# Down products of a feed-forward in three fp32r passes, their operands split on ACT and VectorE

## The chip, the cores and the metric

One core of one Trainium2 chip runs one program: a small perceiver layer, in fp32 throughout. The metric is the device time of one execution in microseconds, the median of several. The engines are PE (TensorE, the matrix engine), DVE (VectorE), ACT (ScalarE), POOL (GpSimd) and SP (SyncE, which issues DMAs here). Each runs its own instructions in order and waits for semaphores that the others raise.

## What is computed

The input `x` is 8 x 64 tokens of 512 numbers. Three blocks follow one another, each added to its input: a cross attention to a context of 8 x 1601 rows; a block with a differential attention over the heads of each token and a feed-forward; a mixture of 32 experts. The change lies in the feed-forward of the second block, whose core is:

```python
h = _layernorm(x, ln1_g, ln1_b)
src2 = _diff_attn(h, Wq, Wk, Wv, lq1, lq2, lk1, lk2, Wo, bo)
conn = skip + src2
skip2 = conn
h2 = _layernorm(conn, ln2_g, ln2_b)
src3 = jax.nn.relu(h2 @ W1.T + b1) @ W2.T + b2
return skip2 + src3
```

`W1` leads from 512 to 2048 numbers ("up"), `W2` back from 2048 to 512 ("down").

## The kernel before

The 512 tokens are 4 tiles of 128. `queries_and_cross_attention` computes the first block, and with it the attention of the second block for tiles 0 to 2. `last_head_and_feed_forward` then has two strands at once: that attention for tile 3 (the "last head"), and the feed-forward for all four tiles. `route_and_experts` follows behind a barrier of all engines.

**The last head.** PE makes `q`, `k` and `v` of tile 3, and ACT copies them out. 24 products follow (`NQ` = 16 of `q` with `k`, `NA` = 8 of the attention weights with `v`), each 128x1024, each reduced by DVE (`reduce`). Two of three products are computed by POOL (`product`, three buffers, so that product m waits for the reduction of m - 3 of its own), one by DVE itself (`vprod`). Between the 16 and the 8 stands a softmax: DVE (`z1`, maxima), ACT (`Exp`), DVE (sums, `rinv`, `rlam`), POOL (`w01`, `att2`). Behind the 8 come a mean square, `on` on POOL, its transposes and product on PE (`turn_o(3)`, `put_out(3)`).

**The feed-forward.** For tile t, DVE adds the attention's output and computes statistics (`connect(t)`), then the normalised rows `cn` (`connection_normed(t)`). PE transposes them (`turn_c(t)`), and ACT scales them into `cT` (`turned_c(t)`). `up(n)`, for n = 16 t + f, makes the f-th 128 hidden numbers of tile t with four fp32 products of 128x128; four of them fill a bank of PSUM. ACT turns a bank into `fT` with four relus (`hidden(n)`), in a ring of 8 places. `down(n)` is one fp32 product of 128x512, with `fT[:, n % 8]` as the stationary operand and a slab of `W2` as the moving one. 16 of them add up to a tile's output, and DVE adds them to `x` (`second_skip(t)`).

**The order** is written out by hand for each engine. PE runs n from 0 to 69: `up(n)`, then `down(n - 6)` (`LAG`), with `turn_c(1)`, `turn_c(2)`, `turn_o(3)`, `put_out(3)` and `turn_c(3)` put in at n = 6, 18, 34, 37 and 43. DVE runs the 24 reductions with `connect` and `connection_normed` of tiles 0 and 1 and `connect(2)` between the first; `connection_normed(2)` stands behind the softmax's maxima, those of tile 3 at the end.

**Memory.** Thirteen weight slabs of 1 MB are loaded once: 0 is `W_O`, 1 to 3 are `Wq`, `Wk` and `Wv` of the last head, 4 is `Wo`, the odd ones from 5 are parts of `W1` and the even ones from 6 parts of `W2`. Slabs 1 to 8 lie in a region called `spare`, 9 to 12 in `h_late`. Elsewhere the kernel has long used three fp32r passes in place of an fp32 product (`mm3`): each operand is split into a high part, rounded to fp32r, and a low part, what that leaves; high x high, high x low and low x high are added up.

Of the kernel before, what the change touches and what calls it, by code (L numbers as in the profile page):

```python
# [19 lines left out]
P = 128  # L20
# [3 lines left out]
TT = T // P  # L24
# [1034 lines left out]
def last_head_and_feed_forward(nc, a, keep):  # L1059
# [12 lines left out]
    with ExitStack() as ctx:  # L1072
# [6 lines left out]

        late = sb("h_late", [P, 4, KD, D])  # L1080
        row, row_loaded = keep["rows"], keep["row_loaded"]
        cols2, b1 = sb("h_cols2", [P, 2, KD]), sb("h_b1", [P, FT])
# [7 lines left out]
        cT = sb("h_cT", [P, 2, KD, P])  # L1090
        fT = sb("h_fT", [P, NF_, P])
        ps = ctx.enter_context(nc.psum_tensor("ps_h", [P, 8, 512], F32))
        UP = 5
# [20 lines left out]
        cT_full, cT_done, up_full, f_done = sem("h_cT_full"), sem("h_cT_done"), sem("h_up_full"), sem("h_f_done")  # L1114
        down_full, skip_done, x2_done = sem("h_down_full"), sem("h_skip_done"), sem("h_x2_done")

        block = ctx.enter_context(nc.Block())
# [80 lines left out]
        def _(act):  # L1198
# [15 lines left out]
            def turned_c(t):  # L1214
# [6 lines left out]
                ins.then_inc(cT_done, 1)  # L1221

            def hidden(n):
                f = n % FT
                act.wait_ge(up_full, n - f % 4 + 4)
                if n >= NF_:
                    act.wait_ge(down_full, n - NF_ + 1)
                c = slice(P * (f % 4), P * (f % 4) + P)
                nc.scalar.activation(fT[:, n % NF_], ps[:, UP + n // 4 % 2, c], ACT.Relu, bias=b1[:, f:f + 1]).then_inc(f_done, 1)

            for t in range(HT):
                turned_o(t)
            act.wait_ge(n_step, 5)
            nc.scalar.activation(std2[:, :, HT:], var2[:, :, HT:], ACT.Sqrt).then_inc(n_std_done, 1)
# [5 lines left out]
            query_key(0)  # L1240
            query_key(1)
            act.wait_ge(qkv_full, 3)
            nc.scalar.copy(v.rearrange("p d h -> p h d"), ps[:, 4].rearrange("p (h d) -> p h d", h=H2)).then_inc(qkv_done, 1)
            act.wait_ge(c_loaded, 32)
            std_second(0)
            turned_c(0)
            std_second(1)
            for n in range(4 * FT):
# [21 lines left out]
        def _(dve):  # L1270
            def reduce(n):
                what, i = kind(n)
                out, width = (att, 4 * H2) if what == "qk" else (o, 4 * D2)
                if n in by_pool:
                    m = by_pool.index(n)
                    summed = prod[:, m % NP]
                    dve.wait_ge(prod_done, m + 1)
                else:
                    m = by_vector.index(n)
                    summed = vprod[:, m % NPV]  # L1280
                    if m >= NPV:
                        dve.wait_ge(red_done, by_vector[m - NPV] + 1)
                    operands_ready(dve, n)
                    multiply(nc.vector, n, summed).then_inc(vprod_done, 1)
                    dve.wait_ge(vprod_done, m + 1)
                nc.vector.tensor_reduce(out[:, width * i:width * i + width], summed.rearrange("p (a d) -> p a d", d=D2), AX.X,
                                        ALU.add).then_inc(red_done, 1)

            def normed_once(t):
# [50 lines left out]
            connect(0)  # L1340
            normed_once(HT)
            for n in range(NQ):
                reduce(n)
                if n == 0:
                    connection_normed(0)
# [4 lines left out]
                if n == 7:  # L1350
                    connect(2)

            dve.wait_ge(red_done, NQ)
# [16 lines left out]
            dve.wait_ge(rsum_step, 2)  # L1370
            nc.vector.tensor_scalar(rlam[:], rinv[:, H2:], lam[:], None, ALU.mult).then_inc(rsum_step, 1)
            for n in range(NQ, NQ + NA):
                reduce(n)
            dve.wait_ge(sq_done, 1)
            nc.vector.tensor_reduce(ms[:], sq.rearrange("p (a d) -> p a d", a=H2), AX.X, ALU.add).then_inc(ms_step, 1)
# [4 lines left out]
            dve.wait_ge(rms_done, 1)  # L1380
            nc.vector.reciprocal(rrms[:], rms[:]).then_inc(ms_step, 1)
            connect(3)
            connection_normed(3)
            second_skip(1)
            second_skip(2)
            second_skip(3)

        @block.tensor
        def _(pe):
# [59 lines left out]
            def down(n):  # L1449
# [8 lines left out]
                if f % 4 == 0:  # L1458
                    pe.wait_ge(w_loaded[6 + 2 * (f // 4)], 16)
                pe.wait_ge(f_done, n + 1)  # L1460
                nc.tensor.matmul(bank, fT[:, n % NF_], weight(6 + 2 * (f // 4))[:, f % 4], start=False, stop=(f == FT - 1)
                                 ).then_inc(down_full, 1)

# [618 lines left out]
def build(nc, a):  # L2082
# [7 lines left out]
    with ExitStack() as ctx:  # L2090
# [5 lines left out]
        with ExitStack() as own:  # L2096
# [28 lines left out]
            keep["w_loaded"] = [nc.alloc_semaphore(f"h_w_loaded{i}") for i in range(NSLAB)]  # L2125
            keep["x_loaded"], keep["tiles_loaded"] = nc.alloc_semaphore("h_x_loaded"), nc.alloc_semaphore("h_tiles_loaded")
            queries_and_cross_attention(nc, a, keep)
            last_head_and_feed_forward(nc, a, keep)
# [63 lines left out]
```

## Time and profile before

| | us |
|---|---|
| median of 3 runs | 1512.81 |
| lowest and highest | 1511.21, 1514.98 |
| the profiled execution in all | 1515.2 |
| its span in the trace | 1513.1 |
| PE busy in the span | 1439.7 |
| DVE busy | 929.3 |
| POOL busy | 655.9 |
| ACT busy | 630.6 |

The profile is of one execution; all times below are microseconds from the start of its span. `last_head_and_feed_forward` takes from about 1001 to 1170. L numbers are lines of the kernel before. A row of the timeline gives the start, the time to the end of its last instruction, the engine and line, the operation and its operands (out<-in), the count, and in brackets how long the engine had been idle before it and who released it. An fp32 product is recorded as two matmuls, so "x2" is one down product and "x8" one `up`. Matmuls overlap in the records: the pace is read from one start to the next.

### The profile page before, as it was taken

Reading aid. Unit: us, or ns where it says so; the run is one execution under the profiler, and the core shown is the slowest. Engines: PE = TensorE matmul, PEld = TensorE weight load, DVE = VectorE, ACT = ScalarE, POOL = GpSimd, SP = SyncE. Lnnn points to the kernel's source line nnn. Section 1 sums busy time; section 2 is a strip of 40 time slices with the busy share of each in tenths; the row PEclk is TensorE's granted clock in tenths of the full one; section 3 lists DMA queues with packets and bytes.
Section 4 is the critical chain, followed back from the end, with each engine's and each line's share of the span. In section 5 each row is a group of like instructions: output and inputs, shape, how many; then the busy total and the mean of one; then the engine's idle time right before and its main releaser. Section 6 shows DMA issues by size and latency. Waiting matters only on the chain. (4 is left out here: it accounts for less than half of the span.)

```text
span 1513.1 us, 24256 instructions
## 1 busy us (share of the span) xinstructions
PE 1439.7 (95%) x8998; PEld 1223.4 (81%) x8998; DVE 929.3 (61%) x2102; ACT 630.6 (42%) x1067; POOL 655.9 (43%) x320
## 2 busy tenths in 40 slices
PE   5999999999999999999999999879999999999993
PEld 4999999989899989899998999845666556777772
DVE  6455555544487655478674459757800557888884
ACT  3344345354343444433534434422211125666662
POOL 5006006005284712464930636427600037888873
PEclk9999999999999999999999999989999799999997
DMA  5102003013002012100201300270000579999999
GB/s 200 64 5 91 1 5 127 2 38 119 29 5 89 11 67 95 60 4 23 77 32 70 107 14 1 98 305 2 1 1 2 199 300 281 370 365 367 370 365 316
DMA packets 63975, 176.96 MB, mean 117 GB/s; under 512 B 15110, under 2 KB 32006, under 8 KB 54028
## 3 DMA queue, kind: packets, MB, share of 16 engines
q1 hardware_dynamic: 53708, 151.57, 27.0%
q0 software_dynamic: 10176, 24.12, 6.5%
q8 instruction: 64, 1.05, 0.3%
q14 instruction: 27, 0.22, 0.0%
HBM read 156.00 MB, written 19.66 MB: 116 GB/s over the span
## 5 line engine op out<-in xcount | busy, mean ns | idle before, releaser
L65 PE MATMUL ps_x<-wkv_hi,c_hi 128*128 128x256 f32 (+1 forms) x832 | 241.2, 290 | 0.0
L294 POOL TENSOR_TENSOR c_hi<-c_raw,ones 128x1608 fp32r<-128x1608 f32 x31 | 90.0, 2904 | 344.7 <-DMA c_raw<-ctxT 344.7
L67 PE MATMUL ps_x<-wkv_hi,c_lo 128*128 128x256 f32 (+1 forms) x832 | 234.2, 282 | 0.0
L66 PE MATMUL ps_x<-wkv_lo,c_hi 128*128 128x256 f32 (+1 forms) x832 | 234.2, 281 | 0.0
L769 DVE TENSOR_TENSOR pT<-ps_x,pT 128x512 fp32r<-128x512 f32 (+1 forms) x224 | 145.2, 648 | 123.2 <-ACT pT L617 120.5
L65 PE MATMUL ps_x<-c_hi,wkv_hi 128*128 128x402 f32 x512 | 195.7, 382 | 3.0 <-POOL c_lo L297 2.4
L617 ACT CAST pT<-ps_x 128x512 fp32r<-128x512 f32 (+1 forms) x224 | 124.5, 556 | 167.4 <-PE ps_x L472 164.3
L598 ACT CAST vv<-ps_x 128x512 fp32r<-128x512 f32 (+1 forms) x112 | 62.1, 555 | 278.5 <-PE ps_x L67 278.5
L67 PE MATMUL ps_x<-c_hi,wkv_lo 128*128 128x402 f32 x512 | 177.9, 347 | 0.0
L66 PE MATMUL ps_x<-c_lo,wkv_hi 128*128 128x402 f32 x512 | 177.7, 347 | 0.0
L65 PEld LDWEIGHTS ps_x<-wkv_hi,c_hi 128*128 128x128 f32 (+1 forms) x832 | 153.5, 184 | 17.0 <-issue 17.0
L739 DVE TENSOR_TENSOR vv<-ps_x,vv 128x512 fp32r<-128x512 f32 (+1 forms) x112 | 72.9, 651 | 139.3 <-ACT vv L598 139.3
L313 POOL TENSOR_TENSOR x_tok<-t_q,t_k 128x1024 f32<-128x1024 f32 x48 | 114.2, 2399 | 100.8 <-PE ps_x L524 58.0
L67 PEld LDWEIGHTS ps_x<-wkv_hi,c_lo 128*128 128x128 f32 (+1 forms) x832 | 153.6, 185 | 0.0
L66 PEld LDWEIGHTS ps_x<-wkv_lo,c_hi 128*128 128x128 f32 (+1 forms) x832 | 153.2, 184 | 0.0
L487 PE MATMUL ps_x<-pT,vv 128*128 128x256 f32 (+1 forms) x832 | 138.1, 287 | 4.8 <-DVE pT L769 4.5
L733 DVE SCALAR_TENSOR_TENSOR kT_lo<-ps_x,bk,kT_hi 128x402 fp32r<-128x402 f32 x128 | 81.1, 635 | 95.7 <-ACT kT_hi L592 95.3
L487 PEld LDWEIGHTS ps_x<-pT,vv 128*128 128x128 f32 (+1 forms) x832 | 125.9, 189 | 10.5 <-DVE pT L769 7.6
L752 DVE TENSOR_SCALAR_CACHE_REDUCE prob<-ps_x 128x402 f32<-128x402 f32 (+1 forms) x256 | 131.1, 569 | 0.0
L472 PE MATMUL ps_x<-ident,prob 128*128 128x128 f32 (+1 forms) x832 | 127.8, 273 | 0.0
L297 POOL TENSOR_TENSOR c_lo<-c_raw,c_hi 128x1608 fp32r<-128x1608 f32 x31 | 115.3, 3720 | 2.4
L1697 POOL DMA_INDIRECT acc<-e_mix,e_row_out x42 | 96.0, 2286 | 34.6 <-issue 31.4
(322 smaller groups left out, 3063.3 us busy)
## 6 DMA issues: line engine op xcount, KB each, us to landing
e_gu_raw<-w_gu SPq DMA_DIRECT2D x49, 1024.0 KB
c_raw<-ctxT SPq DMA_DIRECT2D x32, 804.0 KB
e_w_dn<-w_dn SPq DMA_DIRECT2D x48, 512.0 KB
x_tok<-slabs SPq DMA_DIRECT2D x13, 1024.0 KB, 4.8
spare<-slabs SPq DMA_DIRECT2D x8, 1024.0 KB, 11.2
h_late<-slabs SPq DMA_DIRECT2D x4, 1024.0 KB, 16.6
e_mix<-shared SPq DMA_DIRECT2D x2, 1536.0 KB, 8.7
wkv_raw<-w_qkv SPq DMA_DIRECT2D x2, 1024.0 KB, 12.4
```

The source lines that it names most:

```text
L65: nc.tensor.matmul(out, a_hi, b_hi, start=start, stop=False)
L66: nc.tensor.matmul(out, a_hi, b_lo, start=False, stop=False)
L67: return nc.tensor.matmul(out, a_lo, b_hi, start=False, stop=stop)
L294: nc.gpsimd.tensor_tensor(c_hi[:, :, chunk(c)], c_raw[:, :, chunk(c)], ones[:, 0:1].unsqueeze(2).to_broadcast([P, KD, CW]), ALU.mult).then ...
L297: nc.gpsimd.tensor_tensor(c_lo[:, :, chunk(c)], c_raw[:, :, chunk(c)], f32(c_hi[:, :, chunk(c)]), ALU.subtract).then_inc(split_done, 1)
L313: nc.gpsimd.tensor_tensor(slab[:, 2 * D * (i % 2):2 * D * (i % 2) + 2 * D].rearrange("p (a b d) -> p a b d", a=2, b=2 * H2), q[:, 2 * i:2 ...
L472: ins = nc.tensor.transpose(ps[0:r, 6 + n % 2, c:c + P], prob[:, 2 * g + j, P * st:P * st + r], ident[:])
L487: ins = nc.tensor.matmul(ps[:, 4 + g, 256 * j:256 * j + 256], vv[0:r, st, 2 * g + j].rearrange("p l c -> p (l c)"), pT[0:r, n % 2, st % 2, ...
L617: nc.scalar.copy(pT[0:r, n % 2, 0:w, :, 0].rearrange("p a j c -> p (a j) c"), ps[0:r, 6 + n % 2, 0:256 * w].rearrange("p (a c) -> p a c", ...
L752: ins = nc.vector.tensor_scalar(prob[:, p, CW * n:CW * n + w], ps[:, 2 * (i % 2) + j, 0:w], 0.0, None, ALU.add, ALU.max, accum_out=pmax[:, ...
L769: nc.vector.tensor_tensor(pT[0:r, n % 2, 0:w, :, 1].rearrange("p a j c -> p (a j) c"), ps[0:r, 6 + n % 2, 0:256 * w].rearrange("p (a c) -> ...
L1697: nc.gpsimd.indirect_dma_start(out=a[f"acc{r % 2}"], out_offset=bass.IndirectOffsetOnAxis(ap=row_out[:, r % U:r % U + 1], axis=0), in_=y[: ...
```

## The change

The 64 down products become `mm3`, 192 fp32r passes. For that:

- Each of the four slabs of `W2` is split once. ACT copies it to `down_hi` (`split_down`, 128x2048), DVE subtracts (`down_lo`). `down_lo` takes the slab's own place. Three of the `down_hi` take the places of slabs 1 to 3, `Wq`, `Wk` and `Wv`, as soon as their products are done (`qkv_full`); the fourth has a place of its own.
- `fT` is split in groups of four: ACT copies four tiles to `fT_hi` behind the four relus, DVE subtracts them to `fT_lo` (`hidden_low(G)`, 128x512), G = 0 to 15.
- `down(n)` waits, at the first of each four, for `down_lo` and for `fT_lo` of its group, no longer for the single relu.

Its core, with the new waits and all places of the new calls:

```diff
+        down_hi = [down_hi_0] + [keep["down_hi"][i] for i in range(3)]
+        down_lo = [keep["down_lo_6"], keep["down_lo_8"]] + [
+            nc.alloc_sbuf_tensor_at(f"h_down_lo_{s}", [P, KD, D], F32R, offset=late_at + 4 * KD * D * (s - 9)) for s in (10, 12)]
...
+            def split_down(i):
+                if i:
+                    act.wait_ge(qkv_full, i)
+                act.wait_ge(w_loaded[6 + 2 * i], 16)
+                nc.scalar.copy(down_hi[i][:], weight(6 + 2 * i)).then_inc(down_hi_done, 1)
...
                 nc.scalar.activation(fT[:, n % NF_], ps[:, UP + n // 4 % 2, c], ACT.Relu, bias=b1[:, f:f + 1]).then_inc(f_done, 1)
+                if f % 4 == 3:
+                    s = slice(n % NF_ - 3, n % NF_ + 1)
+                    act.wait_ge(f_done, n + 1)
+                    nc.scalar.copy(fT_hi[:, s], fT[:, s]).then_inc(f_hi_done, 1)
 
             for t in range(HT):
                 turned_o(t)
+            split_down(0)
...
             query_key(0)
             query_key(1)
+            split_down(1)
...
             std_second(0)
             turned_c(0)
+            split_down(2)
+            split_down(3)
             std_second(1)
...
+            def split_down(i):
+                dve.wait_ge(down_hi_done, i + 1)
+                nc.vector.tensor_tensor(down_lo[i][:], weight(6 + 2 * i), f32(down_hi[i][:]), ALU.subtract).then_inc(down_lo_done, 1)
+
+            def hidden_low(G):
+                s = slice(4 * (G % 2), 4 * (G % 2) + 4)
+                dve.wait_ge(f_hi_done, G + 1)
+                nc.vector.tensor_tensor(fT_lo[:, s], fT[:, s], f32(fT_hi[:, s]), ALU.subtract).then_inc(f_lo_done, 1)
...
             normed_once(HT)
+            split_down(0)
             for n in range(NQ):
                 reduce(n)
+                if n in (0, 2, 4):
+                    split_down(n // 2 + 1)
                 if n == 0:
                     connection_normed(0)
...
+                if n in (5, 9, 12):
+                    hidden_low((5, 9, 12).index(n))
...
+            hidden_low(3)
             for n in range(NQ, NQ + NA):
                 reduce(n)
+                if n in (NQ, NQ + 3):
+                    hidden_low(4 + (n - NQ) // 3)
+            hidden_low(6)
...
             nc.vector.reciprocal(rrms[:], rms[:]).then_inc(ms_step, 1)
+            hidden_low(7)
+            hidden_low(8)
             connect(3)
+            hidden_low(9)
             connection_normed(3)
             second_skip(1)
-            second_skip(2)
+            for G in range(10, 4 * TT):
+                hidden_low(G)
+                if G == 12:
+                    second_skip(2)
             second_skip(3)
...
                 if f % 4 == 0:
-                    pe.wait_ge(w_loaded[6 + 2 * (f // 4)], 16)
-                pe.wait_ge(f_done, n + 1)
-                nc.tensor.matmul(bank, fT[:, n % NF_], weight(6 + 2 * (f // 4))[:, f % 4], start=False, stop=(f == FT - 1)
-                                 ).then_inc(down_full, 1)
+                    pe.wait_ge(down_lo_done, f // 4 + 1)
+                    pe.wait_ge(f_lo_done, n // 4 + 1)
+                mm3(nc, bank, fT_hi[:, n % NF_], fT_lo[:, n % NF_], down_hi[f // 4][:, f % 4], down_lo[f // 4][:, f % 4],
+                    False, f == FT - 1).then_inc(down_full, 1)
```

The engines' rows show where the new instructions stand. First DVE, from the first reduction of the last head to `cn` of tile 1 (`h_prod` are POOL's products, `h_vprod` DVE's, `h_y` the connection's sum), before:

```order
L1286 TENSOR_REDUCE t_att<-h_prod 128x64
L1307 RECIPROCAL h_crstd<-h_cstd 128x1
L1311 TENSOR_SCALAR h_cn<-h_y,h_cmv,h_crstd 128x512
L1286 TENSOR_REDUCE t_att<-h_prod 128x64
L1137 TENSOR_TENSOR h_vprod<-t_q,t_k 128x1024
L1286 TENSOR_REDUCE t_att<-h_vprod 128x64
L1286 TENSOR_REDUCE t_att<-h_prod 128x64
L1297 TENSOR_TENSOR h_y<-ps_h,h_y 128x512
```

and in the changed kernel:

```order
L1311 TENSOR_REDUCE t_att<-h_prod 128x64
L1316 TENSOR_TENSOR down_lo_56<-spare,down_hi_52 128x2048
L1341 RECIPROCAL h_crstd<-h_cstd 128x1
L1345 TENSOR_SCALAR h_cn<-h_y,h_cmv,h_crstd 128x512
L1311 TENSOR_REDUCE t_att<-h_prod 128x64
L1148 TENSOR_TENSOR h_vprod<-t_q,t_k 128x1024
L1311 TENSOR_REDUCE t_att<-h_vprod 128x64
L1316 TENSOR_TENSOR h_down_lo_11970<-h_late,down_hi_53 128x2048
L1311 TENSOR_REDUCE t_att<-h_prod 128x64
L1331 TENSOR_TENSOR h_y<-ps_h,h_y 128x512
```

A subtraction of 128x2048 stands now between the first reduction and `cn` of tile 0, and one more ahead of the third reduction of a product of POOL. Next DVE behind the softmax, where the products with `v` are reduced, before:

```order
L1371 TENSOR_SCALAR t_rlam<-t_rinv,t_lam 128x16
L1286 TENSOR_REDUCE t_k<-h_prod 128x64
L1140 TENSOR_TENSOR h_vprod<-t_att,t_v 128x1024
L1286 TENSOR_REDUCE t_k<-h_vprod 128x64
L1286 TENSOR_REDUCE t_k<-h_prod 128x64 x2
```

and in the changed kernel:

```order
L1410 TENSOR_SCALAR t_rlam<-t_rinv,t_lam 128x16
L1321 TENSOR_TENSOR h_fT_lo<-h_fT,h_fT_hi 128x512
L1311 TENSOR_REDUCE t_k<-h_prod 128x64
L1321 TENSOR_TENSOR h_fT_lo<-h_fT,h_fT_hi 128x512
L1151 TENSOR_TENSOR h_vprod<-t_att,t_v 128x1024
L1311 TENSOR_REDUCE t_k<-h_vprod 128x64
L1311 TENSOR_REDUCE t_k<-h_prod 128x64 x2
L1321 TENSOR_TENSOR h_fT_lo<-h_fT,h_fT_hi 128x512
```

The groups 3, 4 and 5 of `fT` stand between the reductions. Last PE, at the change from slab 6 to slab 8 in tile 0, where an `up` (L1445, now L1494) and a down product alternate, before:

```order
L1445 MATMUL ps_h<-h_cT,h_late 128x128 x4
L1461 MATMUL ps_h<-spare,h_fT 128x512
L1445 MATMUL ps_h<-h_cT,h_late 128x128 x4
L1461 MATMUL ps_h<-spare,h_fT 128x512
L1445 MATMUL ps_h<-h_cT,h_late 128x128 x4
```

and in the changed kernel:

```order
L1494 MATMUL ps_h<-h_cT,h_late 128x128 x4
L65 MATMUL ps_h<-h_down_hi,h_fT_hi 128x512
L66 MATMUL ps_h<-down_lo_55,h_fT_hi 128x512
L67 MATMUL ps_h<-h_down_hi,h_fT_lo 128x512
L1494 MATMUL ps_h<-h_cT,h_late 128x128 x4
L65 MATMUL ps_h<-down_hi_52,h_fT_hi 128x512
L66 MATMUL ps_h<-down_lo_56,h_fT_hi 128x512
L67 MATMUL ps_h<-down_hi_52,h_fT_lo 128x512
```

Three passes take the place of each fp32 product, and their order among the `up` is as it was.

## Rows read from the trace of the kernel before

**Rows 1.** Busy time by stretch: stretch, length, then each engine's busy time, clock, DMA.
```profile
1046.00:1073.00 27.00, 23.62 (x130) 16.65 (x131) 26.12 (x25) 6.56 (x17) 14.93 (x7) 0.98 0.01 1
...
1098.00:1170.00 72.00, 71.35 (x365) 47.36 (x363) 4.26 (x9) 12.21 (x42) 1.27 (x1) 1.00 0.00 1
```

**Rows 2.** Timeline of the tensor engine at the transpose of tile 2.
```profile
1072.28 1.12 PE L1430 MATMUL ps_h<-ident,h_cn 128*128 128x128 f32 x4 [3.38 <-DVE h_cn L1311]
```

**Rows 3.** Timeline of the vector engine at the four points named.
```profile
1029.71 1.22 DVE L1286 TENSOR_REDUCE t_att<-h_prod 128x64 f32<-128x1024 f32 x1 [10.40 <-POOL h_prod L1137]
...
1071.68 0.55 DVE L1311 TENSOR_SCALAR h_cn<-h_y,h_cmv,h_crstd 128x512 f32<-128x512 f32 x1
...
1079.16 1.22 DVE L1286 TENSOR_REDUCE t_k<-h_prod 128x64 f32<-128x1024 f32 x1 [4.59 <-POOL h_prod L1140]
...
1092.77 1.22 DVE L1286 TENSOR_REDUCE t_k<-h_vprod 128x64 f32<-128x1024 f32 x1
```

**Rows 4.** Timeline of the tensor engine: a down product, then an `up`.
```profile
1050.36 1.02 PE L1461 MATMUL ps_h<-spare,h_fT 128*128 128x512 f32 x2
1051.22 1.05 PE L1445 MATMUL ps_h<-h_cT,h_late 128*128 128x128 f32 x8
```

**Rows 5.** The same in the query projection, fp32r passes: the first and the 33rd.
```profile
32.69 0.40 PE L65 MATMUL ps_x<-q_xnT_hi,q_wq_hi 128*128 128x512 f32 x1
...
39.97 0.39 PE L67 MATMUL ps_x<-q_xnT_hi,q_wq_lo 128*128 128x512 f32 x1
```

**Rows 6.** The same in the experts, fp32r passes behind fp32 transposes.
```profile
1262.96 0.48 PE L65 MATMUL ps_e<-e_gu_hi,e_xT_hi 128*128 128x512 f32 x1
1263.28 0.39 PE L66 MATMUL ps_e<-e_gu_lo,e_xT_hi 128*128 128x512 f32 x1
1263.51 0.39 PE L67 MATMUL ps_e<-e_gu_hi,e_xT_lo 128*128 128x512 f32 x1
```

**Rows 7.** Timelines of ACT and the vector engine: splits of 128x2048 at the start.
```profile
11.89 1.90 ACT L705 CAST wkv_hi<-wkv_raw 128x2048 fp32r<-128x2048 f32 x1 [4.43 <-DMA wkv_raw<-w_qkv]
...
15.97 2.29 DVE L992 TENSOR_TENSOR wkv_lo<-wkv_raw,wkv_hi 128x2048 fp32r<-128x2048 f32 x1
18.18 2.48 DVE L995 TENSOR_TENSOR q_xnT_lo<-ps_x,q_xnT_hi 128x512 fp32r<-128x512 f32 x4
```

**Rows 8.** Timeline of ACT: `k`, `v` and the first four relus.
```profile
1026.20 1.07 ACT L1207 ACTIVATE t_k<-ps_h 128x512 f32<-128x512 f32 x1 [2.37 <-PE ps_h L1420]
1029.64 1.03 ACT L1243 COPY t_v<-ps_h 128x512 f32<-128x512 f32 x1 [2.37 <-PE ps_h L1420]
...
1043.01 1.14 ACT L1229 ACTIVATE h_fT<-ps_h,h_b 128x128 f32<-128x128 f32 x4 [3.11 <-PE ps_h L1445]
```

**Rows 9.** Timelines of ACT and the vector engine: operations of 128x512.
```profile
16.69 0.58 ACT L713 CAST q_xnT_hi<-ps_x 128x512 fp32r<-128x512 f32 x1
...
1095.94 0.69 DVE L1316 TENSOR_TENSOR x_tok<-ps_h,x_tok 128x512 f32<-128x512 f32 x1
1096.55 0.24 DVE L1381 RECIPROCAL t_rrms<-t_rms 128x16 f32<-128x16 f32 x1
```

**Rows 10.** Timelines of the vector engine and GpSimd: products of 128x1024.
```profile
1033.32 2.23 DVE L1137 TENSOR_TENSOR h_vprod<-t_q,t_k 128x1024 f32<-128x1024 f32 x1
...
1091.52 1.21 DVE L1140 TENSOR_TENSOR h_vprod<-t_att,t_v 128x1024 f32<-128x1024 f32 x1
...
1031.95 2.52 POOL L1137 TENSOR_TENSOR h_prod<-t_q,t_k 128x1024 f32<-128x1024 f32 x1
1034.44 3.33 POOL L1137 TENSOR_TENSOR h_prod<-t_q,t_k 128x1024 f32<-128x1024 f32 x1
```

**Rows 11.** Timeline of the tensor engine: `down(24)`.
```profile
1097.32 1.02 PE L1461 MATMUL ps_h<-h_late,h_fT 128*128 128x512 f32 x2
```

**Rows 12.** Groups of instructions by line: count | busy us, mean ns | idle before.
```profile
L1137 DVE TENSOR_TENSOR h_vprod<-t_q,t_k 128x1024 f32<-128x1024 f32 x5 | 12.8, 2551 | 0.0
...
L1140 DVE TENSOR_TENSOR h_vprod<-t_att,t_v 128x1024 f32<-128x1024 f32 x3 | 5.6, 1865 | 0.0
```

More of the change, by code:

```diff
@@ L1080, in last_head_and_feed_forward @@
         late = sb("h_late", [P, 4, KD, D])
+        late_at = nc.sbuf_base - 4 * 4 * KD * D
+        down_hi_0 = sb("h_down_hi", [P, KD, D], F32R)
         row, row_loaded = keep["rows"], keep["row_loaded"]
@@ L1091, in last_head_and_feed_forward @@
         fT = sb("h_fT", [P, NF_, P])
+        fT_lo = nc.alloc_sbuf_tensor_at("h_fT_lo", [P, NF_, P], F32R, offset=nc.sbuf_base - 4 * NF_ * P)
+        fT_hi = sb("h_fT_hi", [P, NF_, P], F32R)
         ps = ctx.enter_context(nc.psum_tensor("ps_h", [P, 8, 512], F32))
@@ L1115, in last_head_and_feed_forward @@
         down_full, skip_done, x2_done = sem("h_down_full"), sem("h_skip_done"), sem("h_x2_done")
+        f_hi_done, f_lo_done = sem("h_f_hi_done"), sem("h_f_lo_done")
+        down_hi_done, down_lo_done = sem("h_down_hi_done"), sem("h_down_lo_done")
+        down_hi = [down_hi_0] + [keep["down_hi"][i] for i in range(3)]
+        down_lo = [keep["down_lo_6"], keep["down_lo_8"]] + [
+            nc.alloc_sbuf_tensor_at(f"h_down_lo_{s}", [P, KD, D], F32R, offset=late_at + 4 * KD * D * (s - 9)) for s in (10, 12)]
         block = ctx.enter_context(nc.Block())
@@ L2126, in build @@
             keep["x_loaded"], keep["tiles_loaded"] = nc.alloc_semaphore("h_x_loaded"), nc.alloc_semaphore("h_tiles_loaded")
+            keep["down_hi"] = [nc.alloc_sbuf_tensor_at(f"down_hi_{i}", [P, KD, D], F32R, offset=top - 4 * size + 4 * KD * D * i) for i in range(3)]
+            keep["down_lo_6"], keep["down_lo_8"] = (
+                nc.alloc_sbuf_tensor_at(f"down_lo_{s}", [P, KD, D], F32R, offset=top - 4 * size + 4 * KD * D * (s - 1)) for s in (6, 8))
             queries_and_cross_attention(nc, a, keep)
```

## The prediction

> **What bounds the kernel now.** I read the profile in four steps. The busy time by stretch comes first: the change touches only 1010 to 1170 us, and there the tensor engine is busy 71.35 of 72 us behind 1098, but only 23.62 of 27 between 1046 and 1073, where the vector engine has 26.12 of 27 [rows 1]. Second, the tensor engine's timeline says who is late: it stops for 3.38 us at 1068.9 and goes on at 1072.28 with the transpose of `cn` of tile 2, released by the vector engine [rows 2]. Third, the vector engine's timeline: from 1029.71 to 1071.68 one instruction follows the other, then it idles 4.59 us for GpSimd's first product behind the softmax, and its last reduction of the head starts at 1092.77 [rows 3]. So two engines take turns: the vector engine sets the pace up to the softmax of the last head, the tensor engine from there on. A saving on the tensor engine counts only behind the last point at which it waits for the vector engine, and work added to the vector engine ahead of that point counts in full.
>
> **What is removed on the tensor engine.** A down product in fp32 takes from 1050.36 to 1051.22: 0.86 us [rows 4]. Its three fp32r passes have rows in the query projection: 32 steps of 128x512 from 32.69 to 39.97, 0.2275 us each [rows 5], so 3 x 0.2275 = 0.68. The saving is 0.177 us a product, 11.3 us for 64, if nothing else stood in the way. Changing from fp32 to fp32r might cost something: behind transposes the first pass of a group takes 0.32, the next 0.23 [rows 6], 0.09 more. The same stretch is also what is left over from the transposes ahead of it, so I take 0, with 0.09 as the upper end; the lower end is 0 too, since no row has a pass under its 0.2275.
>
> The Trainium skill has another price: "TensorE: Matmul & The Clock Gate", section "Back-to-back issue gap", gives pairs of weight load and product a sustained 131 ns at 512 columns. By that a down product would take 0.39 us and the 64 would save 30 us. The trace disagrees with 227.5 ns over 32 steps [rows 5], and I go by the trace; what the page's price would do to the time stands among the rivals.
>
> **What is added, and where.**
> 1. Four weight splits. ACT copies 128x2048 in 1.90 us; the vector engine's subtraction of that shape takes 2.29, and the next instruction starts 2.21 behind it [rows 7]. On ACT the first two lie in idle time: the second fits between 1027.3, the end of `k`, and 1029.64, when `v` begins [rows 8]; copies 2 and 3 follow the turned `c` of tile 0. All are done before the vector engine asks, by 0.4 us at the closest. The DMAs are those of before. On the vector engine subtraction 0 lies in its idle time ahead of 1029.71 [rows 3] and costs nothing. Subtractions 1 to 3 stand behind the reductions 0, 2 and 4, where the engine has no gap: 3 x 2.21 = 6.63 us. `cn` of tiles 0 and 1 is queued behind them, and the tensor engine behind `cn`.
> 2. Sixteen splits of `fT`, in fours. ACT: the group of four relus is 1.14 us [rows 8], a copy of 128x512 adds 0.58. The vector engine: 128x512 with 0.61 to the next [rows 9]. Three stand ahead of `cn` of tile 2: 1.83 us. Group 3 falls into the idle 4.59 us [rows 3]. Groups 4 and 5 stand between the reductions: 1.22. Groups 7 to 15 meet an idle engine. GpSimd has no new instruction.
> 3. Waits. `down(4G)` now waits for the vector engine's in-order queue, with all later `up` behind it. In steady state there are three `up` and three `down` between group G's last `up` and its first `down`, some 4.6 us, against 1.14 + 0.58 + 0.69 and some 0.2 of signals: no wait. At the end no `up` is left: 3 x 0.68 + 0.1 against 2.6 to 2.9, a new wait of 0.7. And `put_out(3)` waits for a copy on ACT now one copy later: 0.3.
>
> **The shared lock.** A subtraction with both inputs in SBUF does not run beside a GpSimd product. The vector engine's product takes 1.21 us alone (1091.52) but 2.23 at 1033.32, when GpSimd's of 1031.95 is running; and GpSimd's next, of 1034.44, takes 3.33 where 2.3 is usual, longer by just what the vector engine held [rows 10]. So each new subtraction waits for a running product of GpSimd, and pushes the next. I walked both queues with these durations, each asking when free and the first to ask being served. The same walk through the kernel before gives the end of the stage within 0.7 us of the trace. The changed one: subtraction 1 is asked at 1030.9 and waits 1.0; `cn` of tile 0 meets the next product (1.4 more than before) and is ready at 1036.8; subtraction 2 waits 0.9; subtraction 3 none, but the vector engine's product behind it 2.2 (0.7 more); `cn` of tile 1 0.7 less than before, ready at 1056.0, for which the tensor engine idles from 1047.3, nearly 9 us; `fT` group 2 waits 1.0; the last product ahead of the softmax 1.1 less; small ones make up 0.2 less. Together 3.0. So `cn` of tile 2 moves by 6.63 + 1.83 + 3.0 = 11.4 us, from 1071.68 to 1083.1.
>
> Behind it: group 3 holds up GpSimd's `w01` by 0.5; group 4 takes 0.61 + 1.0 of wait, group 5 0.61 + 1.2; the vector engine's products gain 1.2 and lose 0.9. Sum 4.2, so the last reduction starts at 1092.77 + 15.6 = 1108.4. Group 6 stands behind it: 1108.4 + 1.13 + 0.69 + 0.05 = 1110.2, and `down(24)`, which started at 1097.32 [rows 11], must wait for that. It moves by **12.9 us**. At half the tensor clock behind the long waits (at 1072.28 four transposes take 1.12 us [rows 2]) there is a loss of some 1.5 us as before, ahead of this point and covered by it.
>
> **The sum.** From `down(24)` on the tensor engine leads: 40 products save 40 x 0.177 = 7.1 us, against 0.7 and 0.3 of new waits. 12.9 - 7.1 + 1.0 = +6.8 us. What follows the stage starts behind a barrier and only shifts. The profiled execution had a span of 1513.1 and 1515.2 us in all; it becomes 1519.9 and 1522.0. On the median of 1512.81 that is **1519.6 us**, 0.45% slower.
>
> **Rivals.**
> - *No new lock waits.* If the added work only filled time that the lock costs already, and new waits cancelled, the shift at the last reduction would be 6.63 + 1.83 + 1.22 + 0.5 = 10.2 instead of 15.6, the end +1.4: 1514.2. The vector engine's eight products lose 12.8 + 5.6 - 8 x 1.21 = 8.7 us to the lock today [rows 12], which can move either way. Chance 0.18, counted as no change.
> - *The other side: GpSimd gets ahead.* Each subtraction delays the vector engine's products while GpSimd's buffers fill, so later ones could find the lock free. The shift at the last reduction must fall below 4.3 us for a gain over 0.3%, so 5.9 of the 8.7 us must vanish. If all vanish, the shift is 1.5, the tensor engine waits no longer than today, and 64 products less 1.0 of waits give about -10: 1502.5. Against it: GpSimd's queue is bound to the reductions by three buffers, so it is late together with them. Chance 0.05.
> - *Cheaper passes.* Under 0.133 us a pass, the 40 products would give back over 18.4 us and win by over 0.3%. By the skill's page above it would be 0.131 and about 1508. Every row of 512 columns at full clock says 0.23. Chance 0.01.
> - *Costly change of type.* 0.09 us for each product behind `down(24)`: +3.6, so 1523.2. Only the first passes behind transposes speak for it. Chance 0.13.
> - *My walk:* 0.63, 1516 to 1523.
>
> **How the numbers follow.** About 0.3% (4.5 us) is what a measurement of this kernel can tell from no change. Slower by more begins at 1517.3. The costly change and most of my walk lie above: 0.13 + 0.58 = 0.71. No change: 0.18 + 0.05 of the walk = 0.23. Faster: 0.06. The range takes in the bare durations (1514.2, less 1.7 for errors of the walk) and at the top the change of type with 2.3 us more of lock wait, one product of GpSimd: 1512.5 to 1525.5.
>
> **What would show it.** The four subtractions at 2.3 to 3.3 us; tensor idle time of 8 to 9 us ahead of `cn` of tile 1 and of some 5 ahead of tile 2, a total of 16 to 20 in the stage; `down` pairs at 1.57 us instead of 1.75 behind 1110; vector idle time still near 4.5 behind the softmax. I am wrong if the tensor engine reaches `down(24)` before 1106 or waits for `fT_lo` in steady state, or if a pass takes over 0.25 us.

## The result

The changed kernel took 1521.96 us (median of 4 runs, 1521.27 to 1524.41) against 1512.38 us of the kernel before (4 runs, with one more than was shown ahead of the prediction): a ratio of 1.0064, 95% interval 1.0046 to 1.0081. It is slower by 9.6 us, forecast were 6.8. The kernels were run side by side twice more below, with differences of the medians of 9.3 and 8.7 us. Over all runs the medians are 1522.12 (11 runs) and 1514.12 (32), 8.0 us apart; that figure is lower than each of the three because the series have unequal shares in the two medians.

The profiled execution had a span of 1519.1 us and took 1521.27 us. The first lines of its page, busy time and share of the span by engine:

```profile
span 1519.1 us, 24427 instructions
...
PE 1432.8 (94%) x9062; PEld 1237.5 (81%) x9062; DVE 953.8 (63%) x2122; ACT 648.1 (43%) x1087; POOL 661.3 (44%) x320
```

The tensor engine works 7 us less than before and the span is longer. The same stretches as in [rows 1], and the one between them, say where the time is lost (stretch, length, then busy time of PE, PEld, DVE, ACT, POOL, the granted clock, DMA):

```profile
1046.00:1073.00 27.00, 19.00 (x103) 16.09 (x104) 26.74 (x24) 7.76 (x20) 18.14 (x9) 0.75 0.00 1
1073.00:1098.00 25.00, 21.19 (x130) 18.14 (x129) 19.77 (x20) 7.64 (x20) 15.54 (x10) 0.93 0.00 1
1098.00:1170.00 72.00, 69.49 (x444) 59.22 (x443) 21.06 (x29) 19.98 (x56) 5.92 (x4) 1.00 0.00 1
```

PE has 19.00 us of work in 1046 to 1073 where it had 23.62, beside a DVE that is as full as before. Its timeline has the waits, in brackets:

```profile
1034.99 0.66 PE L1479 MATMUL ps_h<-ident,h_cn 128*128 128x128 f32 x4 [2.39 <-DVE h_cn L1345]
...
1054.00 1.12 PE L1479 MATMUL ps_h<-ident,h_cn 128*128 128x128 f32 x4 [8.32 <-DVE h_cn L1345]
...
1081.93 0.90 PE L1479 MATMUL ps_h<-ident,h_cn 128*128 128x128 f32 x4 [3.38 <-DVE h_cn L1345]
...
1084.96 0.77 PE L65 MATMUL ps_h<-down_hi,h_fT_hi 128*128 128x512 f32 x1 [0.42 <-DVE h_fT_lo L1321]
...
1100.86 0.48 PE L65 MATMUL ps_h<-down_hi,h_fT_hi 128*128 128x512 f32 x1 [1.41 <-DVE h_fT_lo L1321]
...
1108.49 0.47 PE L65 MATMUL ps_h<-down_hi,h_fT_hi 128*128 128x512 f32 x1 [1.03 <-DVE h_fT_lo L1321]
```

All are on DVE. The first three are the transposes of tiles 0, 1 and 2. The last three are the down products 12, 20 and 24, which wait for the low part of `fT` of the groups 3, 5 and 6. The counterpart of the last is [rows 11].

The stage starts 1.7 us earlier in this execution than in the one before, because half the granted clock lasted 6.8 us instead of 10.2 ahead of it. So places are compared from the first addition of the stage on DVE, at 1011.12 before and 1009.44 after (its row: `t_x<-ps_h`):

| from the stage's first addition, us | before | after | later by | forecast |
|---|---|---|---|---|
| `cn` of tile 1 | 33.7 | 44.0 | 10.3 | |
| `cn` of tile 2 | 60.6 | 71.9 | 11.3 | 11.4 |
| last reduction of the last head | 81.7 | 97.1 | 15.4 | 15.6 |
| `down(24)` | 86.2 | 99.1 | 12.9 | 12.9 |
| last addition to `x` | 158.3 | 165.7 | 7.4 | 6.8 |

These are DVE's rows at those points (of the rows of before, [rows 3]) and the two ends:

```profile
1009.44 0.69 DVE L1357 TENSOR_TENSOR t_x<-ps_h,t_x 128x512 f32<-128x512 f32 x1 [6.10 <-PE ps_h L1518]
...
1081.33 0.55 DVE L1345 TENSOR_SCALAR h_cn<-h_y,h_cmv,h_crstd 128x512 f32<-128x512 f32 x1
...
1106.53 1.22 DVE L1311 TENSOR_REDUCE t_k<-h_vprod 128x64 f32<-128x1024 f32 x1
...
1175.18 0.69 DVE L1350 TENSOR_TENSOR x_tok<-ps_h,x_tok 128x512 f32<-128x512 f32 x1 [3.27 <-PE ps_h L67]
```

And these are new operations on DVE and two old ones behind them, in the order in which they stand (not among them are weight split 0, 2.29 us in idle time, and the groups 0, 3 and 6 of `fT`, 0.68 or 0.69 us each). `down_lo` is a weight split (2.29 alone, [rows 7]), `h_fT_lo` one of a group of `fT` (0.69 alone); what is longer has waited for the lock:

```profile
1029.20 3.27 DVE L1316 TENSOR_TENSOR down_lo<-spare,down_hi 128x2048 fp32r<-128x2048 f32 x1
...
1032.58 2.35 DVE L1345 TENSOR_SCALAR h_cn<-h_y,h_cmv,h_crstd 128x512 f32<-128x512 f32 x1
...
1039.40 3.20 DVE L1316 TENSOR_TENSOR h_down_lo<-h_late,down_hi 128x2048 fp32r<-128x2048 f32 x1
...
1046.50 2.28 DVE L1316 TENSOR_TENSOR h_down_lo<-h_late,down_hi 128x2048 fp32r<-128x2048 f32 x1
1048.70 3.34 DVE L1148 TENSOR_TENSOR h_vprod<-t_q,t_k 128x1024 f32<-128x1024 f32 x1
...
1063.85 0.69 DVE L1321 TENSOR_TENSOR h_fT_lo<-h_fT,h_fT_hi 128x512 fp32r<-128x512 f32 x1
...
1070.18 1.68 DVE L1321 TENSOR_TENSOR h_fT_lo<-h_fT,h_fT_hi 128x512 fp32r<-128x512 f32 x1
...
1090.36 1.70 DVE L1321 TENSOR_TENSOR h_fT_lo<-h_fT,h_fT_hi 128x512 fp32r<-128x512 f32 x1
...
1098.78 1.94 DVE L1321 TENSOR_TENSOR h_fT_lo<-h_fT,h_fT_hi 128x512 fp32r<-128x512 f32 x1
```

The pace of the tensor engine behind `down(24)` stands in its timeline, from one `up` (L1494) to the next 1.59 us (1.585 over several), where an `up` and a down product took 1.75 before:

```profile
1109.26 1.05 PE L1494 MATMUL ps_h<-h_cT,h_late 128*128 128x128 f32 x8
1110.07 0.48 PE L65 MATMUL ps_h<-down_hi,h_fT_hi 128*128 128x512 f32 x1
1110.38 0.39 PE L66 MATMUL ps_h<-h_down_lo,h_fT_hi 128*128 128x512 f32 x1
1110.61 0.39 PE L67 MATMUL ps_h<-down_hi,h_fT_lo 128*128 128x512 f32 x1
1110.85 1.05 PE L1494 MATMUL ps_h<-h_cT,spare 128*128 128x128 f32 x8
```

### The profile page after: what moved, and what is told of

It is laid out like the page before. It is cut to its first block and busy times, and to the rows that moved or that the text cites. A ratio compares the mean times of both kernels' runs of the same rounds, so it can differ in the third digit from the quotient of the medians.

```text
span 1519.1 us, 24427 instructions
## 1 busy us (share of the span) xinstructions
PE 1432.8 (94%) x9062; PEld 1237.5 (81%) x9062; DVE 953.8 (63%) x2122; ACT 648.1 (43%) x1087; POOL 661.3 (44%) x320
```

## The experiments

The theory is the one of the prediction: one queue, DVE's, sets the pace up to the subtraction of `fT` group 6, the lock with GpSimd is part of it, and only behind it the cheaper products pay. Lines with + and - stand against the changed kernel. "From the first addition" is measured as in the table above.

### The changed kernel again

> The changed kernel as it is, again beside the kernel before. The profiles put the stage 7.4 us longer (down(24) 12.9 us later and 5.5 us won back behind it, after taking off a start that was 1.7 us earlier in the profile after), the medians put the whole 9.6 us longer. Theory A: the stage is all there is, the rest is scatter of the start and end of the program: the difference of medians comes out between 7 and 8.5 us. Rival B: some 2 us more are lost in every run outside the stage: it stays at 9 to 10 us, and another profile shows where.

Measured: 1523.62 us (5 runs) against 1514.37 (17 runs), ratio 1.0064 (1.0051 to 1.0078): 9.3 us. By this difference theory A (7 to 8.5 us) falls; the medians over all runs, 8.0 us apart, lie within it, but they mix the series unequally. Rival B looked for the rest outside the stage. What the new profile has more lies inside it: 167.1 us from the first to the last addition instead of 165.7, and behind the last addition it is 2.0 us shorter (341.9 instead of 343.9). Up to `cn` of tile 1 the two profiles agree within 0.1 us. Then group 1 of `fT` takes 2.88 us on DVE instead of 0.69. The two timelines side by side, first the profile on record (ACT's copy, GpSimd's product, DVE's subtraction):

```profile
1063.20 0.62 ACT L1250 CAST h_fT_hi<-h_fT 128x512 fp32r<-128x512 f32 x1
...
1063.91 6.17 POOL L1148 TENSOR_TENSOR h_prod<-t_q,t_k 128x1024 f32<-128x1024 f32 x2 [3.54 <-DVE t_att L1311]
```

and the repeat:

```profile
1064.59 0.62 ACT L1250 CAST h_fT_hi<-h_fT 128x512 fp32r<-128x512 f32 x1
...
1065.19 2.37 POOL L1148 TENSOR_TENSOR h_prod<-t_q,t_k 128x1024 f32<-128x1024 f32 x1 [3.55 <-DVE t_att L1311]
...
1065.24 2.88 DVE L1321 TENSOR_TENSOR h_fT_lo<-h_fT,h_fT_hi 128x512 fp32r<-128x512 f32 x1
```

The reduction ahead of it frees a buffer for GpSimd at the same moment as it lets DVE go on. On record the copy is ready at 1063.82, DVE asks at 1063.85, 0.06 us ahead of GpSimd, and waits for nothing. In the repeat the copy is ready at 1065.21, GpSimd asks at 1065.19, and DVE, 0.05 us behind, waits for the whole product: 2.2 us. ACT's copy is later because half the granted clock holds until 1064.5 here, 53.8 us behind the first addition, instead of 52.3. The later products then fall otherwise (one on DVE runs 1.21 instead of 2.26), and 1.3 us are left at `cn` of tile 2.

### One weight split in idle time

```diff
             query_key(0)
+            split_down(1)
             query_key(1)
-            split_down(1)
...
             split_down(0)
+            split_down(1)
             for n in range(NQ):
                 reduce(n)
-                if n in (0, 2, 4):
+                if n in (2, 4):
```

> The changed kernel, but subtraction 1 of the weight splits stands ahead of the first reduction of the last head, where the vector engine idles for 8.2 us (its copy on ACT stands between q and k). Theory (the vector engine's queue up to fT group 6 sets the pace, and the lock is part of it): 2.2 us of work and the waits around it (1.0, and 1.4 at cn of tile 0) go, 3.5 to 4.5 us less than the changed kernel, so 3 to 5 us over the kernel before; down(24) 9 us later than before instead of 12.9. Rival (the work on the vector engine is not what costs, but the coarser waits of the tensor engine for groups of four): no change from the changed kernel, within 1 us.

Measured: 1518.93 us (6 runs), ratio 1.0033 (1.0021 to 1.0046); 4.6 us over the kernel before and 4.7 under the changed kernel beside it. In its profile the moved subtraction takes 2.29 us in idle time and `cn` of tile 0 is 2.8 us earlier. The last addition comes at 163.7 us from the first: 2.1 less than on record, 3.4 less than the repeat above, which lost the same race for group 1 as this one did. `down(24)` is 10.8 us later than before where I had expected 9: `cn` of tile 1 is 3.4 us earlier than on record, but the lost race takes 1.3 us of that back. The rival, that the queue does not matter, is out. A weight split that is moved 5 us ahead, with no instruction less, gives back 2 to 3 us of the stage in the profiles and 4.7 of 9.3 us in the medians.

### Without the subtractions of `fT`

```diff
             def hidden_low(G):
-                s = slice(4 * (G % 2), 4 * (G % 2) + 4)
-                dve.wait_ge(f_hi_done, G + 1)
-                nc.vector.tensor_tensor(fT_lo[:, s], fT[:, s], f32(fT_hi[:, s]), ALU.subtract).then_inc(f_lo_done, 1)
+                return
...
-                    pe.wait_ge(f_lo_done, n // 4 + 1)
+                    pe.wait_ge(f_hi_done, n // 4 + 1)
-                mm3(nc, bank, fT_hi[:, n % NF_], fT_lo[:, n % NF_], down_hi[f // 4][:, f % 4], down_lo[f // 4][:, f % 4],
+                mm3(nc, bank, fT_hi[:, n % NF_], fT_hi[:, n % NF_], down_hi[f // 4][:, f % 4], down_lo[f // 4][:, f % 4],
```

> The changed kernel without the 16 subtractions of fT: the third pass reads the high part again, so the low part of fT is left out of the result. The copies on ACT and the passes are all there; the tensor engine waits for the copy. Theory: cn of tile 2 comes 1.6 to 1.8 us earlier than in the changed kernel, the last reduction 5 to 6 us earlier, and the end 5 to 6.5 us earlier, so 1 to 3 us over the kernel before. Rival (the coarse waits cost little and only the weight splits matter): 1 to 2 us less than the changed kernel.

Measured: 1513.82 us (11 runs), ratio 1.0000 (0.9991 to 1.0009): level with the kernel before, 9.8 us under the changed kernel beside it. `cn` of tile 2 is 2.7 us earlier than in the profile on record, the last reduction 6.8, the last addition 7.5. Each is more than I had forecast (1.6 to 1.8, 5 to 6, 5 to 6.5). Five of the subtractions stand ahead of the last reduction outside idle time, 3.05 us at 0.61 each; the other 3.7 us are waits for the lock, their own, those of the products behind them, and GpSimd's. So five small subtractions put off the last reduction by more than twice their own time, and without the sixteen the stage is as long as before (158.2 against 158.3). The difference of the medians is 2.3 us more than that of the profiles. The race for group 1, which this kernel does not run, can be part of it, and so can the time behind the stage: 340.0 us in this profile, 343.9 on record.

### Three passes only for tiles 2 and 3

```diff
+                if n < 32:
+                    if f % 4 == 0:
+                        pe.wait_ge(w_loaded[6 + 2 * (f // 4)], 16)
+                    pe.wait_ge(f_done, n + 1)
+                    nc.tensor.matmul(bank, fT[:, n % NF_], weight(6 + 2 * (f // 4))[:, f % 4], start=False, stop=(f == FT - 1)
+                                     ).then_inc(down_full, 1)
+                    return
...
             nc.vector.reciprocal(rrms[:], rms[:]).then_inc(ms_step, 1)
-            hidden_low(7)
+            for i in range(3):
+                split_down(i)
             hidden_low(8)
             connect(3)
+            split_down(3)
             hidden_low(9)
```

(ACT copies the slabs ahead of `hidden(20)` and `hidden(24)`, DVE subtracts once the fp32 product that reads a slab last is done; the groups 0 to 7 of `fT` are not split.)

> Only the down products of tiles 2 and 3 in three passes, those of tiles 0 and 1 in fp32 as before; the four weight splits and all subtractions of fT stand behind the last reduction of the last head, where the vector engine idles. Theory: nothing moves up to down(32), from there 32 products save 0.165 us each, 5.3 us, less 0.7 to 1.0 of new waits at the end: 4 to 5 us less than the kernel before, 0.27 to 0.33%. Rival (the passes cost more than they look beside fp32 products, or the four splits are late and hold up down(32)): no gain, within 1 us of the kernel before or slower.

Measured: 1509.26 us (6 runs), ratio 0.9966 (0.9953 to 0.9978): 5.1 us faster than the kernel before and 14.4 us faster than the changed one beside it. This version beats both. From the first addition, `cn` of tile 2 and the last reduction stand where they stood before (60.6 and 81.7), and the last addition comes at 152.6 instead of 158.3. Not all of these 5.8 us are the passes. The transposes of tile 2 come at 61.2 us from the first addition in both, behind the same wait of 3.38 us, but before they ran at half the granted clock ([rows 2]: 1.12 us) and here they do not, and `down(24)` comes at 84.8 instead of 86.2:

```profile
1072.70 0.66 PE L1479 MATMUL ps_h<-ident,h_cn 128*128 128x128 f32 x4 [3.38 <-DVE h_cn L1346]
...
1096.35 1.02 PE L1511 MATMUL ps_h<-h_late,h_fT 128*128 128x512 f32 x2
```

That is 1.4 us by the clock alone, in the profile of the kernel before (3.4 us at half, from 1071.8). The other 4.4 us come behind `down(32)`, within the 4 to 5 that were expected. Its tensor engine at the first product in three passes, `down(32)`, which begins without a wait:

```profile
1112.84 1.05 PE L1494 MATMUL ps_h<-h_cT,spare 128*128 128x128 f32 x8
1113.73 1.02 PE L1511 MATMUL ps_h<-h_late,h_fT 128*128 128x512 f32 x2
1114.59 1.05 PE L1494 MATMUL ps_h<-h_cT,spare 128*128 128x128 f32 x8
1115.58 1.12 PE L1506 MATMUL ps_h<-spare,ones 1*128 1x512 f32 x2
1116.63 0.50 PE L65 MATMUL ps_h<-h_down_hi,h_fT_hi 128*128 128x512 f32 x1
```

### The tensor engine kept busy in its waits

```diff
-                pe.wait_ge(cn_done, t + 1)
                 pe.wait_ge(qkv_done, min(t, 2) + 1)
+                pe.wait_ge(w_loaded[5], 16)
+                for _ in range((2, 9, 3, 0)[t]):
+                    nc.tensor.matmul(ps[:, CN_BANK[t]], ident[:], weight(5)[:, 0], start=True, stop=True)
+                pe.wait_ge(cn_done, t + 1)
```

> The changed kernel with 2, 9 and 3 more fp32 products of 128x512 on the tensor engine while it waits for cn of tiles 0, 1 and 2 (into banks that the transposes behind them overwrite, so the result stays the same). In the changed kernel the wait of 5 to 8 us for tile 1 is followed by 7 to 10 us at half the granted clock, and a second spell of 3 to 7 us follows the wait for tile 2; the profile of the first repeat has the last reduction 1.3 us later than the profile on record, with longer spells. Theory A (half clock makes the tensor engine late, and so the groups of fT and the vector engine behind it): the granted clock stays at full from 1010 on, the stage is 1 to 2.5 us shorter than in the changed kernel. Rival B (the vector engine's queue covers the slow spells, the scatter is that of the lock alone): within 0.7 us of the changed kernel.

Measured: 1521.09 us (6 runs) against 1514.06 (11 runs), ratio 1.0045 (1.0031 to 1.0059). The granted clock is at full from 1010 to 1181 us in its profile, where the changed kernel had 1048.1 to 1061.7 at half and 1082.2 to 1085.6 again. The same stretches as above:

```profile
1046.00:1073.00 27.00, 24.82 (x133) 17.88 (x131) 26.67 (x25) 8.17 (x22) 18.15 (x8) 1.00 0.00 1
1073.00:1098.00 25.00, 21.20 (x125) 16.98 (x126) 19.77 (x20) 7.64 (x20) 15.75 (x9) 1.00 0.00 1
```

All the same the last addition comes at 165.75 us, as on record (165.74), and `cn` of tile 2 at 71.9 in both. So half the clock by itself costs the changed kernel nothing on record: DVE's queue covers it, as B says. (In the kernel before, where the tensor engine leads from tile 2 on, a spell of 3.4 us cost 1.4 us, as seen above.) What it can do is make ACT's copy of group 1 late. Here the copy is ready at 1062.1, more than 3 us ahead of DVE, and the race is not run. With the filler the stage of the repeat, 1.3 us longer, could not come about by that way. The medians are 1.0 us (against all 11 runs) to 2.5 us (against the five) lower, which is more than the 0.7 us of B; but behind the last addition, too, this profile is 3.6 us shorter than the one on record (340.3 against 343.9). That the race makes part of the scatter is shown by the traces of single executions; its mean price is not measured.

### One more subtraction

```diff
+                if n == 4:
+                    dve.wait_ge(down_hi_done, 4)
+                    nc.vector.tensor_tensor(xt[:], weight(12), f32(down_hi[3][:]), ALU.subtract)
                 if n in (0, 2, 4):
                     split_down(n // 2 + 1)
```

> The changed kernel with one more subtraction of 128x2048 on the vector engine ahead of split 3, between the reductions 4 and 5, into the place of slab 0, whose contents nobody needs by then. Theory (one queue, every microsecond on it up to fT group 6 counts): cn of tile 1 and tile 2, the last reduction and the end are all later by 2.2 us, plus or minus a changed lock wait of up to 2.3; so 1.5 to 4.5 us more than the changed kernel. Rival (there is slack between the vector engine and the tensor engine): less than 1 us more.

Measured: 1524.58 us (4 runs), ratio 1.0066 (1.0051 to 1.0081), 2.5 us over the median of all runs of the changed kernel. In its profile `cn` of tile 1 is 2.2 us later than on record, that of tile 2, the last reduction and the last addition 3.5 us each. 2.2 us are its own, and 1.3 us are left of a longer lock wait for group 1 (2.87 instead of 0.69), as in the repeat. The split 3 behind it now waits 2.1 us for the lock (4.41 instead of 2.28) and DVE's product behind that no longer does (1.21 instead of 3.34), so that this wait has only changed its place. Nothing of the 3.5 us is absorbed by the tensor engine.

### GpSimd's products made small

```diff
-                multiply(nc.gpsimd, n, prod[:, m % NP]).then_inc(prod_done, 1)
+                nc.gpsimd.tensor_tensor(prod[:, m % NP, 0:2], prod[:, m % NP, 0:2], prod[:, m % NP, 2:4], ALU.mult).then_inc(prod_done, 1)
```

> The changed kernel with GpSimd's 16 products of 128x1024 for the last head replaced by products of two columns (the last head's attention is left out to that extent, the result is not the reference's). Theory (the waits of the new subtractions are those for the lock with GpSimd): the subtractions of 128x2048 take 2.29 us each and those of 128x512 0.69 each, all of them, and cn of tile 0 0.55 instead of 2.35. Rival (other traffic in SBUF or the in-place write makes them slow): 3.2 to 3.3 us for subtractions 1 and 2 and 1.7 to 2.9 for some of fT as before.

Its profile, DVE's new operations at the same places as above:

```profile
1028.08 2.29 DVE L1319 TENSOR_TENSOR down_lo<-spare,down_hi 128x2048 fp32r<-128x2048 f32 x1
...
1030.48 0.55 DVE L1348 TENSOR_SCALAR h_cn<-h_y,h_cmv,h_crstd 128x512 f32<-128x512 f32 x1
...
1037.15 2.29 DVE L1319 TENSOR_TENSOR h_down_lo<-h_late,down_hi 128x2048 fp32r<-128x2048 f32 x1 [2.61 <-ACT down_hi L1241]
...
1058.69 0.69 DVE L1324 TENSOR_TENSOR h_fT_lo<-h_fT,h_fT_hi 128x512 fp32r<-128x512 f32 x1 [1.91 <-ACT h_fT_hi L1253]
```

2.29, 2.29 and 2.28 for the weights, 0.55 for `cn` of tile 0, 0.68 or 0.69 for six of the seven groups; only group 2 takes 0.88, beside one of the three additions of 128x512 that GpSimd still has. The rival is out: the extra time of the subtractions goes with GpSimd's products, in all of them. DVE waits 1.9 and 2.6 us for ACT's copies now, since it arrives earlier. The whole took 1548.5 us in its one run; that says nothing, since the time is added behind the stage (378.3 us behind the last addition to `x` instead of 343.9), where other values can send other rows to the experts (not shown).

### The changed kernel a third time

> The changed kernel a third time, for another profile. Theory (lock waits and clock spells fall differently from one execution to the next, by a GpSimd product of 2.3 us here or there): the sum of the lock waits in the nine subtractions between the first and the last reduction differs by up to 2.5 us from the profile on record, and the stage's length with it, 7.4 to 10 us over before. Rival (the stage is always the same and the scatter lies outside it): the stage is within 0.3 us of one of the two profiles.

Measured: 1521.21 and 1524.24 us, ratio 1.0057 (1.0038 to 1.0077), 8.7 us over the kernel before beside it. The profile repeats the one on record within 0.1 us everywhere: `cn` of tile 2 at 71.9, the last addition at 165.76, group 1 in 0.69 us. So of three profiles two are alike and one is 1.3 us longer. The theory named a cause that is real, but its size (up to 2.5 us between executions, a stage of up to 10 us over before) did not show; the stage was 7.4, 8.7 and 7.4 us over before. Behind the last addition the profiles of this case differ by more than that, and with the clock: up to 1480 us, 340.0 and 340.3 us with 17.1 us at half the granted clock (without the subtractions of `fT`, and with the filler), 340.8 and 341.9 with 20.5 (the early split, the first repeat), 343.6 with 23.9 (the kernel before), 343.8 to 345.0 with 27.3 (the rest, without the one with the small products). So a good part of the scatter of the whole lies behind the stage.

## Why the prediction was right

**What bounds the kernel.** Right: the tensor engine waits for DVE up to `down(24)`, and from there it leads. The extra subtraction and the moved one show that work on DVE's queue ahead of that point counts in full: 2.2 us more put off `cn` of tile 1 by 2.2 us, and the stage by those and the changed lock wait.

**The walk of the two queues.** Right, and closer than its range: subtraction 1 waited 0.98 us (1.0 forecast), subtraction 2 0.91 (0.9), subtraction 3 not at all, and the product behind it 2.1 (2.2). `cn` of tile 0 lost 1.1 more than before (1.4), and group 2 waited 1.0 (1.0). `cn` of tile 2 moved 11.3 us (11.4), the last reduction 15.4 (15.6), `down(24)` 12.9 (12.9). The rival without new lock waits would have had 10.2 at the last reduction. The rival in which GpSimd gets ahead had its fall in DVE's products (one lost 2.1 us, another nothing), but the eight of them still lost 8.1 us to the lock, where before it was 8.7 and 5.9 would have had to vanish.

**What is won back.** The term was 7.1 us less 1.0 of new waits, 6.1; measured are 5.45 (12.85 less 7.4). The pace is 1.585 us for an `up` and a down product where I had 0.89 + 3 x 0.2275 = 1.5725: 40 x 0.0125 = 0.5 us of the difference. The first pass behind an `up` shows 0.31 us to the next in its row and the `up` ahead of it only 0.81. By their sum, which is what counts, the change of type costs 0.01 us and not the 0.09 of the costly rival. The waits were there as forecast: at the end the product comes 0.8 us later than the pace (forecast 0.7), at `put_out(3)` 0.2 (0.3). The last 0.15 us of the difference are not traced.

**The skill's price.** The Trainium skill, "TensorE: Matmul & The Clock Gate", section "Back-to-back issue gap", has 131 ns for a pair of weight load and product at 512 columns; here the passes of the down product stand 0.23 us apart, as in [rows 5]. The rival of cheaper passes is out.

**The time.** Forecast were 6.8 us for the stage and for the whole. The stage became 7.4 us longer in two profiles and 8.7 in the third; the whole 9.6, 9.3 and 8.7 us in the three series side by side. The number is right by its range, and the centre is too low by 2 to 3 us. Of these, 0.65 are the term above, and 1.3 come in where the race for group 1 is lost, which the walk did not have. A third part was in the profile that I started from: it has the 3.4 us at half the clock behind tile 2 which cost 1.4 us of its stage. I carried them over "as before", but in the changed kernel DVE sets `down(24)`, clock or no clock. Against an execution of the kernel before without this spell the stage would be 8.8 us longer, an estimate from 7.4 + 1.4. The kernel before has one profile only, so how often it has the spell, and how the 2 to 3 us divide, stays open.

**A wrong detail.** I put the loss by half the clock at 1.5 us "as before". Behind the wait of 8.3 us it lasted 13.65 us, not 3.4. It was covered, as said, but its real effect was not in the walk at all: it moves ACT's copy of group 1 across the moment at which GpSimd asks for the lock.

**The signs.** The tensor engine waited 8.3 us ahead of tile 1 (8 to 9 forecast), but 3.4 and not some 5 ahead of tile 2, since the longer spell at half clock made it late itself. In the whole stage it was idle for 20.0 us (16 to 20), DVE behind the softmax for 4.4 (4.5). `down(24)` came at 1108.5, not before 1106. Ahead of it the tensor engine waited for the groups 3 and 5 as well (0.4 and 1.4 us), which the walk did not list; that costs nothing, because `down(24)` has to wait for DVE all the same. Behind it the only wait for `fT_lo` is the one at the end.

## What to carry to other kernels

Cheaper work on the engine that is busiest pays only where that engine is the last one, so look for the last point at which it waits for another, and count everything that the change puts on that other engine ahead of it. Here the same three passes lost some 9 us when applied to all tiles and won 5 when applied only behind that point. Where two engines share a lock, a small new operation costs its own time and often a large operation of the neighbour; walking both queues, with durations from the profile, gave the lock waits named above within 0.3 us each. One profile is one execution: look what the clock did in it before taking its length as the base of a forecast.

## What the runs showed of the hardware

- The lock between DVE and GpSimd is given for whole instructions to the one that asks first: 0.06 us ahead meant no wait, 0.05 us behind 2.2 us. DVE instructions with two inputs in SBUF took 2.29 us (128x2048) and 0.69 (128x512) without GpSimd's products and up to 4.41 and 2.88 with them. The normalisation of 128x512, one input in SBUF and two scalars a partition, took 0.55 and 2.35, so it takes part in the lock too. By the Trainium skill, "SBUF — State Buffer", section "Who interferes with whom", the pair of ports that DVE shares with GpSimd is an exclusive lock, a DVE instruction with two SBUF inputs contends with a GpSimd instruction that reads SBUF, and (said there of DVE's two-port modes) whoever issues first has the pair for the whole instruction; the traces agree.
- The length of a wait of the tensor engine does not tell what it loses by half the granted clock. Behind the same wait of 3.38 us for tile 2, after the same instructions, the kernel before had 3.4 us at half and the version with three passes for tiles 2 and 3 none, and reached `down(24)` 1.4 us earlier. In two executions of the changed kernel the wait for tile 1 was 8.3 us, followed by 7.7 us more at half the clock while it worked, and 5.0 us, followed by 9.3. The wait was the shorter one because the engine had already run 6.8 us at half ahead of it.
- Fourteen fp32 products without use, put into three waits (2, 9 and 3), kept the clock at full for the whole stage and cost nothing, but won nothing in the stage either, because the engine was not the last one there.
